# Weights turned by f32 transpositions, the first head's weights and tiles first, the experts' weights turned and folded in the first six periods

## The reference

```python
xn = _layernorm(x, axis=-1)                       # x: 8 x 1024 x 128
Q = einsum('bnd,hdk->bhnk', xn, proj_q)           # 8 heads
K = einsum('bmd,dk->bmk', xn, proj_k)
V = einsum('bmd,dv->bmv', xn, proj_v)
weights = softmax(einsum('bhnk,bmk->bhnm', Q, K), axis=-1)
Y = einsum('bhnv,hdv->bnd', einsum('bhnm,bmv->bhnv', weights, V), proj_o)
ffn = einsum('aemn,enh->amh', einsum('amh,ehn->aemn', xn, w1), w2)   # w1: 8 x 128 x 512
out = x + Y + ffn
```

## Time and profile before

| | |
|---|---|
| median of 3 runs | 1669.72 us |
| profiled execution | 1669.67 us, span 1667.9 us |
| ScalarE busy | 1304.2 us (78%) |
| VectorE busy | 1239.3 us (74%) |
| GpSimd busy | 1379.9 us (83%) |
| first matmul | 5.77 us into the span |
| first `high_pass` | 24.92 us |
| DMA | near full for some 30 us, then about 1% |

### The profile page before, as it was taken

The page is one execution under the profiler, slowest core; times in us unless marked ns, Lnnn a source line. Parts: engine busy times, 40 slices in busy tenths (PEclk is TensorE's granted clock), DMA queues, the critical chain, the costliest instruction groups (busy, mean ns, idle before and its releaser), DMA issues.

```text
span 1667.9 us, 46510 instructions
## 1 busy us (share of the span) xinstructions
PE 1634.7 (98%) x18820; PEld 1214.1 (73%) x18820; DVE 1239.3 (74%) x2655; ACT 1304.2 (78%) x1350; POOL 1379.9 (83%) x1008
## 2 busy tenths in 40 slices
PE   7999999999999999999999999999999999999998
PEld 6777777777777777777777777777777777777775
DVE  5777777777777777777777777777777777777775
ACT  4777877787787788778778777877878787787785
POOL 2788888888888888888888888888888888878876
PEclk9999999999999999999999999999999999999999
DMA  8000000000000000000000000000000000000000
GB/s 230 2 2 2 1 2 14 2 2 2 2 15 2 2 2 3 13 2 2 2 8 8 2 2 1 8 8 2 2 2 8 8 2 2 2 14 2 2 1 14
DMA packets 16769, 16.73 MB, mean 10 GB/s; under 512 B 432, under 2 KB 12976, under 8 KB 16560
## 3 DMA queue, kind: packets, MB, share of 16 engines
q1 hardware_dynamic: 15520, 13.24, 2.7%
q10 hardware_dynamic: 1040, 0.52, 0.1%
HBM read 9.57 MB, written 4.19 MB: 8 GB/s over the span
## 4 chain that ended last, share of the span: by engine, by line
POOL 56%; issue 24%; PE 18%; ACT 1%; DVE 0%; POOLq 0%; DMA 0%; SPq 0%; DVEq 0%; ACTq 0%
POOL pr_lo L306 40%; POOL xacc L318 9%; POOL xn L300 3%; PE s_ps L548 2%; PE s_ps L550 2%; PE s_ps L535 2%; PE t_ps L586 2%; PE t_ps L589 2%; PE t_ps L588 2%; POOL rstd L345 2%; POOL xacc L324 1%; POOL xn_lo L290 1%; PE s_ps L432 1%; PE s_ps L434 1%; PE s_ps L433 1%
## 5 line engine op out<-in xcount | busy, mean ns | idle before, releaser
L306 POOL TENSOR_TENSOR pr_lo<-pr,pr_hi 128x1024 f16<-128x1024 f32 x511 | 1086.4, 2134 | 264.3 <-ACT pr_hi L396 264.3
L389 ACT ACTIVATE pr<-s_ps,boost,scale 128x1024 f32<-128x1024 f32 x512 | 616.8, 1205 | 211.1 <-PE s_ps L550 210.3
L778 DVE TENSOR_REDUCE key_max<-s_ps 128x128 f16<-128x1024 f32 x512 | 624.0, 1219 | 0.0
L396 ACT ACTIVATE pr_hi<-pr 128x1024 f16<-128x1024 f32 x512 | 525.4, 1051 | 8.1
L548 PE MATMUL s_ps<-g_lo,xT 128*128 128x128 f16 x4096 | 512.4, 219 | 1.1 <-DVE g_lo L791 1.1
L550 PE MATMUL s_ps<-g_hi,xT 128*128 128x128 f16 x4096 | 512.3, 219 | 0.0
L548 PEld LDWEIGHTS s_ps<-g_lo,xT 128*128 128x128 f16 x4096 | 400.7, 98 | 31.6 <-DVE g_lo L791 1.6
L550 PEld LDWEIGHTS s_ps<-g_hi,xT 128*128 128x128 f16 x4096 | 400.8, 98 | 29.7
L586 PE MATMUL t_ps<-pr_hi,xn_hi 128*128 128x512 f16 x1024 | 388.7, 380 | 16.3 <-POOL pr_lo L306 14.4
L588 PE MATMUL t_ps<-pr_lo,xn_hi 128*128 128x512 f16 x1024 | 388.1, 379 | 0.0
L589 PE MATMUL t_ps<-pr_hi,xn_lo 128*128 128x512 f16 x1024 | 388.1, 379 | 0.0
(11 more groups left out here) (123 smaller groups left out, 1602.7 us busy)
## 6 DMA issues: line engine op xcount, KB each, us to landing
out_dram<-xacc SPq DMA_DIRECT2D x16, 256.0 KB, 2.3
w_sb<-in_L_ffn_w_dram SPq DMA_DIRECT2D x1, 2048.0 KB, 10.2
pr<-in_L_attn_proj_q_dram ACTq DMA_DIRECT2D x1, 512.0 KB, 4.7
xacc<-in_L_attn_x_dram SPq DMA_DIRECT2D x2, 256.0 KB, 5.1
pr<-in_L_attn_proj_o_dram SPq DMA_DIRECT2D x1, 512.0 KB, 6.5
xacc<-in_L_attn_x_dram SPq DMA_DIRECT2D x1, 384.0 KB, 11.0
xacc<-in_L_attn_x_dram SPq DMA_DIRECT2D x1, 128.0 KB, 6.3
wkv<-in_L_attn_proj_k_dram SPq DMA_DIRECT2D x1, 64.0 KB, 2.9
```

The costliest lines, as they stand in the source:

```text
L306: pool.tensor_tensor(pr_lo[:, u % RING, :], pr32[:, u % PR, :], pr_hi[:, u % RING, :], ALU.subtract)\
L389: act.activation(pr32[:, u % PR, :], both_banks(u), ACT.Exp, bias=boost[:, 0:1], scale=scale[:, 0:1])\
L396: act.activation(pr_hi[:, u % RING, :], pr32[:, u % PR, :], ACT.Copy).then_inc(p_hi_ready, 1)
L778: dve.tensor_reduce(key_max[:, u % 2, :], both_banks(u).rearrange("p (t q) -> p q t", q=P), AX_X, ALU.max).then_inc(keys_max, 1)
```

## The change

- Query, output and w1 weights are turned by `pe.transpose` with the f32 identity instead of f32 matmuls. The centring is then done elsewhere: for the query weights on VectorE, which copies the turned first columns of the heads (`wq_first`) and subtracts them while emptying PSUM (ScalarE's copy L368 goes); for the experts once, by one f32 matmul of F with `centre` in period 7, with a second copy of F.
- TensorE's prologue: the output weights are turned behind fold A; fold C is split in two halves, one ahead of `project(0)`, one in period 0; tiles 0 to 3 are turned ahead of `row_of_amax`; tiles 4 to 7 behind `project(0)`; no expert is turned in the prologue.
- ScalarE splits one head of A high first, the other seven behind the first `g_high`; C is copied in two halves. GpSimd makes the low half of tiles 0 to 3 as well. VectorE's order is changed to suit.
- All 8 experts are turned in periods 0 to 3, two in each, through one PSUM bank; all 8 are folded in periods 4 and 5, four in each, in the other bank. F's largest is found in period 8.

```diff
-        def w1_turn(e):
-            return s_ps[:, (2 + e % 2) * BANK:(3 + e % 2) * BANK] if e < 3 else sum_bank(-2)
+        def c_ps(half):
+            return s_ps[:, (2 + half) * BANK:(3 + half) * BANK]
+        W1_BANK, FOLD_BANK = 0, 1
+        FOLDS = {4: 0, 5: 1}
@@ GpSimd
+            first_rstd(0)
+            first_rstd(1)
+            xn_low(0, 0, HT)
             xn_low(HT, HT, HT)
+            first_rstd(2)
@@ ScalarE
-            act.wait_ge(transposed, 2)
-            act.activation(wqT, s_ps[:, 0:N].rearrange("p (h k) -> p h k", h=H), ACT.Copy).then_inc(evacuated, 1)
-            split_high(0, 0, HT)
             act.wait_ge(transposed, 3)
             act.activation(woT, s_ps[:, N:2 * N], ACT.Copy).then_inc(evacuated, 1)
+            split_high(0, 0, HT)
             split_high(HT, HT, HT)
-            act.wait_ge(folded, 2)
-            act.activation(c32[:, :], s_ps[:, N:2 * N], ACT.Copy).then_inc(c_copied, 1)
             act.wait_ge(scales, 1)
-            act.activation(a_hi[:, :, :], a_ps.rearrange("p (h k) -> p h k", h=H), ACT.Copy,
-                           scale=inv_scale[:, 0:1]).then_inc(hi_ready, 1)
-            for e in range(3):
-                empty_w1(e)
+            high_of_a(0, 1)
+            empty_c(0)
             g_high(0)
+            high_of_a(1, H - 1)
+            empty_c(1)
             for n in range(PERIODS):
-                if n < 3:
-                    empty_w1(2 * n + 3)
+                if n < 4:
+                    empty_w1(2 * n)
...
                     exponentials(n - 1)
-                if n < 2:
-                    empty_w1(2 * n + 4)
+                if n < 4:
+                    empty_w1(2 * n + 1)
@@ TensorE
             for h in range(H):
-                last = pe.matmul(s_ps[:, h * P:(h + 1) * P], wq_sb[:, h, :], centre[:, :], start=True, stop=True)
-            last.then_inc(transposed, 1)
-            pe.wait_ge(o_in, 16)
-            for h in range(H):
-                last = pe.matmul(s_ps[:, N + h * P:N + (h + 1) * P], wo_sb[:, h, :], ident[:, :], start=True, stop=True)
+                last = pe.transpose(s_ps[:, h * P:(h + 1) * P], wq_sb[:, h, :], ident[:, :])
             last.then_inc(transposed, 1)
...
             last.then_inc(folded, 1)
+            pe.wait_ge(o_in, 16)
+            for h in range(H):
+                last = pe.transpose(s_ps[:, N + h * P:N + (h + 1) * P], wo_sb[:, h, :], ident[:, :])
+            last.then_inc(transposed, 1)
@@ turn_w1(e)
                 for c in range(MC):
-                    last = pe.matmul(w1_turn(e)[:, c * P:(c + 1) * P], w1_sb[:, e, c * P:(c + 1) * P], centre[:, :],
-                                     start=True, stop=True)
+                    last = pe.transpose(sum_bank(W1_BANK)[:, c * P:(c + 1) * P], w1_sb[:, e, c * P:(c + 1) * P], ident[:, :])
@@ max_to_row(u)
+                if u == 3:
+                    pe.wait_ge(w1_evacuated, E)
@@ chunk(n, place)
+                if n < 4 and rest:
+                    turn_w1(2 * n + place)
+                if n in FOLDS and rest:
+                    for e in range(2):
+                        fold_ffn(4 * FOLDS[n] + 2 * place + e)
@@ small_products(n)
+                if n == F_CENTRED:
+                    pe.wait_ge(f_copied, 1)
+                    pe.matmul(ffn_part(n), centre[:, :], f32w[:, :], start=True, stop=True).then_inc(f_ps, 1)
@@ TensorE's order
-            row_of_amax(0, None)
             turn_tiles(0)
+            row_of_amax(0, None)
             spread_amax(0, None)
-            turn_w1(0)
-            turn_tiles(HT)
-            turn_w1(1)
+            fold_c(0)
             pe.wait_ge(weights_ready, 1)
             project(0)
-            turn_w1(2)
+            turn_tiles(HT)
             for n in range(PERIODS):
...
+                if n == 0:
+                    fold_c(1)
                 chunk(n, 0)
@@ VectorE
             tile_stats(0)
+            wq_turned = s_ps[:, 0:N].rearrange("p (h d) -> p h d", h=H)
+            dve.wait_ge(transposed, 2)
+            dve.tensor_copy(wq_first[:, :], wq_turned[:, :, 0]).then_inc(wq_first_ready, 1)
+            dve.wait_ge(wq_first_ready, 1)
+            dve.tensor_tensor(wqT, wq_turned, wq_first[:, :].unsqueeze(2).to_broadcast([P, H, P]), ALU.subtract)\
+               .then_inc(evacuated, 1)
+            tile_means(0)
             tile_stats(1)
+            tile_means(1)
             normalise_first(0)
...
             dve.wait_ge(folded, 1)
             find_amax(0, a_ps)
+            normalise_first(1, 0, 2)
             reduce_amax(0, None)
+            normalise_first(1, 2, 4)
             power_of_two(0, None)
+            copy_first(0)
             low_of_a(0, 1)
+            tile_stats(2)
+            tile_means(2)
+            copy_first(HT)
```

More of the change, by code:

```diff
@@ L169, in attention_ffn, with first_turned @@
         a_ps = s_ps[:, 4 * BANK:6 * BANK]
-        def w1_turn(e):
-            return s_ps[:, (2 + e % 2) * BANK:(3 + e % 2) * BANK] if e < 3 else sum_bank(-2)
+        def c_ps(half):
+            return s_ps[:, (2 + half) * BANK:(3 + half) * BANK]
+        def first_turned(first):
+            return (t_ps[:, BANK:2 * BANK] if first == 0 else s_ps[:, 3 * BANK:4 * BANK]).bitcast(F16)
         def summing(n):
@@ L239, in ffn_part @@
             return bank(n + 1, 0)[:, 0:D]
+        F_CENTRED = 7
         def turned_part(n):
@@ L279, in _, with first_rstd @@
             pool.memset(centre[0:1, 0:1], 0.0).then_inc(consts, 1)
-            for g, (first, count) in enumerate(FIRST_TILES):
+            def first_rstd(g):
+                first, count = FIRST_TILES[g]
                 pool.wait_ge(ln_var, g + 1)
@@ L364, in empty_w1, with high_of_a, empty_c @@
                 act.wait_ge(w1_turned, e + 1)
-                act.activation(w1T[:, e, :], w1_turn(e), ACT.Copy).then_inc(w1_evacuated, 1)
-            act.wait_ge(transposed, 2)
-            act.activation(wqT, s_ps[:, 0:N].rearrange("p (h k) -> p h k", h=H), ACT.Copy).then_inc(evacuated, 1)
-            split_high(0, 0, HT)
+                act.activation(w1T[:, e, :], sum_bank(W1_BANK), ACT.Copy).then_inc(w1_evacuated, 1)
+            def high_of_a(first, count):
+                heads = a_ps.rearrange("p (h k) -> p h k", h=H)[:, first:first + count, :]
+                act.activation(a_hi[:, first:first + count, :], heads, ACT.Copy, scale=inv_scale[:, 0:1])\
+                   .then_inc(hi_ready, 1)
+            def empty_c(half):
+                act.wait_ge(folded, half + 2)
+                act.activation(c32[:, half * BANK:(half + 1) * BANK], c_ps(half), ACT.Copy).then_inc(c_copied, 1)
             act.wait_ge(transposed, 3)
             act.activation(woT, s_ps[:, N:2 * N], ACT.Copy).then_inc(evacuated, 1)
+            split_high(0, 0, HT)
             split_high(HT, HT, HT)
-            act.wait_ge(folded, 2)
-            act.activation(c32[:, :], s_ps[:, N:2 * N], ACT.Copy).then_inc(c_copied, 1)
             act.wait_ge(scales, 1)
-            act.activation(a_hi[:, :, :], a_ps.rearrange("p (h k) -> p h k", h=H), ACT.Copy,
-                           scale=inv_scale[:, 0:1]).then_inc(hi_ready, 1)
-            for e in range(3):
-                empty_w1(e)
+            high_of_a(0, 1)
+            empty_c(0)
             def g_high(k):
@@ L453, in _, with fold_c @@
             last.then_inc(folded, 1)
[L454 to L458, removed]
+            pe.wait_ge(o_in, 16)
+            for h in range(H):
+                last = pe.transpose(s_ps[:, N + h * P:N + (h + 1) * P], wo_sb[:, h, :], ident[:, :])
+            last.then_inc(transposed, 1)
+            def fold_c(half):
+                pe.wait_ge(evacuated, 2)
+                if half == 1:
+                    pe.wait_ge(xT_ready, NT)
+                pe.matmul(c_ps(half), wkvT[:, P:2 * P], woT[:, half * BANK:(half + 1) * BANK], start=True, stop=True)\
+                  .then_inc(folded, 1)
             def turn_tiles(first):
@@ L515, in high_pass @@
                     if u == 1:
-                        pe.wait_ge(w1_evacuated, 3)
+                        pe.wait_ge(c_copied, 1)
+                    if u == F_CENTRED + 1:
+                        pe.wait_ge(f_copied, 2)
                     if u - 1 in SPREAD:
@@ L596, in fold_ffn @@
                     pe.wait_ge(w1_evacuated, E)
+                    pe.wait_ge(max_found, 4)
+                    pe.wait_ge(bias_ready, 3)
                 for c in range(MC):
-                    last = pe.matmul(sum_bank(-1)[:, 0:D], w1T[:, e, c * P:(c + 1) * P], w2_sb[:, e, c, :],
+                    last = pe.matmul(sum_bank(FOLD_BANK)[:, 0:D], w1T[:, e, c * P:(c + 1) * P], w2_sb[:, e, c, :],
                                      start=e == 0 and c == 0, stop=e == E - 1 and c == MC - 1)
@@ L727, in low_of_a @@
                 heads = a_ps.rearrange("p (h k) -> p h k", h=H)[:, first:first + count, :]
-                dve.wait_ge(hi_ready, 1)
+                dve.wait_ge(hi_ready, 1 if first == 0 else 2)
```

(19 more changed lines are left out.)

49 lines of the change are left out of this document (25 added, 24 removed).

## The result

The changed kernel takes 1672.95 us in the median of 16 runs (1671.16 to 1674.76), the kernel before 1669.18 us (16 runs, 1668.60 to 1670.30). The ratio is 1.0021, 95% interval 1.0014 to 1.0029. The forecast was 1671.3, range 1667.8 to 1674.6. The profiled execution took 1673.30 us, span 1671.5.

What follows compares the result with a forecast made beforehand. TensorE was taken to bound the kernel, with everything decided in the first 50 us. The prologue's -1.2 us and the periods' +2.85 us summed to +1.65 us, giving 1671.3 us, range 1667.8 to 1674.6.

Steps and rivals of the forecast that it cites:

- K: Start of the first reduction over keys, 25.58 us in the kernel before; forecast at 24.4, 1.2 us earlier.
- E(5): Start of unit 5's exponential; its shift is the end's shift. Prediction wrong if it comes before 48 or after 54.
- What bounds, and where the time is decided: Whole kernel: TensorE busy 98% of the span; the steady stretch from 60 us keeps its length, the first 50 us decide.
- Price of an f32 transposition: TensorE's turns of 128 x 128 weights: 0.112 us taken each, between bounds 0.056 and 0.224.
- lower-price rival: Weight turns on TensorE: 0.056 us a transposition, -1.8 us, time 1669.5, with a full clock 1667.7; chance 0.20.
- rival of 0.224 us: Weight turns on TensorE: f32 transposition costs what the f32 product costs, +3.8 us, time 1675.1; chance 0.10.
- Periods 0 to 3 and 4 to 6: After the prologue: first fold at K + 15.3, then TensorE alone for 12.85 us; bunching the folds loses 2.85 us.
- E(0): Start of unit 0's exponential, forecast at K + 5.7; the numbers 1 and 2 mean units 1 and 2, K + 8.95 and 13.25.
- gapless rival: Early periods lose nothing: TensorE's 22.6 us from K to E(5) run without gaps, time 1664; chance 0.06.
- Prologue: Chain of weight work ahead of K: K 3.0 us earlier at 22.6, less 1.8 us for one clock fall.
- Fold A: 1.79, 10.3 to 12.1: Prologue step on TensorE: fold A takes 1.79 us, from 10.3 to 12.1, 1.1 us earlier than before.
- The clock stays low longer: Prologue: fold A at half clock, 1.1 us more, time 1672.4; with a second fall in periods 0 to 3, 1674.1; chance 0.17.

Runs made afterwards that it cites:

- w1_matmul: Changed kernel with w1 turned by f32 matmuls with the identity instead of transpositions; median 1674.92 us, ratio 1.0034 to the kernel before.
- bunched: Kernel before with only the folds' places changed: four in each of periods 4 and 5, none in 2, 3 and 6; median 1670.53 us, ratio 1.0008.
- dve_copies: Changed kernel with the w1 copies of experts 5 and 7 (periods 2 and 3) on VectorE instead of ScalarE; median 1671.81 us, ratio 1.0015.
- fill_start: Changed kernel with only 30 filler matmuls ahead of the key weights' arrival; median 1671.10 us, ratio 1.0009 to the kernel before.
- fill_pause: Changed kernel with only 14 filler matmuls in TensorE's pause between turned query weights and fold A; median 1671.96 us, ratio 1.0015 to the kernel before.
- q_matmul: Changed kernel with the query weights turned by f32 matmuls with the identity, first columns still subtracted on VectorE; median 1672.49 us, ratio 1.0017 to the kernel before.
- before_fill: Kernel before plus filler f16 matmuls: 30 ahead of the key weights, 24 before tiles 4 to 7 are turned; median 1667.65 us, ratio 0.9992.
- fill_matmul: Changed kernel plus 70 f16 filler matmuls: 30 ahead of the key weights, 14 ahead of fold A, 26 ahead of the first tiles' turn; median 1669.03 us.
- w1_only: Kernel before with w1 turned by f32 transpositions in the old places and F centred by one f32 matmul in period 7; median 1668.12 us, ratio 0.9994.

## Why the prediction was right, and where it was off

The time fell inside the stated range, on the forecast side of the kernel before, and periods 0 to 6 went as forecast. The prologue did not: K was to come 1.2 us earlier and came 0.63 later. The range held because its upper part allowed for a longer low clock. The prediction's own sign of being wrong, E(5) after 54, came true by a little (54.30). And 3.8 us is more than the 3.3 that it took as distinguishable, an outcome (slower) to which it gave 0.16.

**What bounds, and where the time is decided: right.** The steady stretch is unchanged, and time less E(5) is constant within 0.5 us over fourteen kernels.

**Price of an f32 transposition: right.** 0.112 taken, 0.111 measured. The Trainium skill (TensorE: Matmul & The Clock Gate, Terms) has the transposition mode four times faster for f32; here it is twice as fast as the f32 matmul (0.224 us), so the lower-price rival is out. So is the rival of 0.224 us: w1_matmul shows what the w1 turns alone would have cost. (By its own terms that rival would pass +3.3 from 0.16 a transposition, not 0.17.)

**Periods 0 to 3 and 4 to 6: right.** K + 5.7, 8.95, 13.25, first fold 15.3, E(5) 28.15 were forecast; 5.63, 9.07, 13.02, 15.14 and 28.09 came. Two errors cancel in part, which is luck: E(0) to E(1) took 3.44 (3.25 forecast), E(1) to E(2) 3.95 (4.3). The loss from K to E(5) is 2.78 us (2.85 forecast). bunched shows 1.25 of it as the folds' place alone. dve_copies gives back 0.63 for two of ScalarE's copies. If the two add up, which was not tried, about 0.9 is left; it would lie in the other turns and copies that the periods took over from the prologue, and was not taken apart further. The gapless rival is out.

**Prologue: mis-sized, by the clock.** The forecast had K at 24.4, 1.2 us ahead of before; it was 26.21, 0.63 behind. The step "Fold A: 1.79, 10.3 to 12.1" is where it went: 10.08 to 13.83. The step took for granted that the clock rises by 8.75 as before; it rose at about 14.4 in the profiled execution. Of the 1.96 us too much, 1.73 is the clock (3.75 against 2.02 at the full clock), and 0.23 is that fold A behind a pause takes 2.02, not 1.79, even then. With the output weights' turn (1.25 against 0.9) TensorE is 2.1 late at 15.08 against the forecast's 13.0, and 1.8 of it is carried on to K. That is the rival "The clock stays low longer", priced there at 1.1 us. The low clock later in the prologue was in the forecast with 1.8 us, for a fall at 15.6, which came at about 17.8. Filling the pauses gives 3.9 us of medians, so about half of what the low clock cost was foreseen.

**The mechanism behind that rival: not as named.** It leaned on transpositions not holding the clock. The Trainium skill (TensorE: Matmul & The Clock Gate, Part 4) says so; for f16 transpositions the runs disagree (1669.13 with them, 1669.03 with matmuls, and fold A at full speed behind 30 of them). What the runs show is that more work of TensorE ahead of fold A has the clock up for it: 30 fillers at the start (fill_start), 14 in the pause (fill_pause), or the longer query turn of q_matmul with no filler and the pause left open, fold A 2.02 in each. So the pause alone is not what kept the clock low; it was the pause together with how little ran ahead of it. Whether an f32 transposition counts less than an f32 matmul of the same length was not tried by itself, and stays open.

**The sum.** +1.65 was forecast, +3.6 to +3.8 measured: 0.6 from the prologue, 2.8 from the periods, and 0.2 in the profiled executions that no part here accounts for (twelve other kernels do not show it).

## What to carry to other kernels

A kernel that TensorE bounds is shortened by taking work off TensorE only where nothing else sets the pace. Work moved from a prologue into periods must meet idle time of the same engine there, and heavy pieces were better spread than bunched here (1.25 us). In a prologue of short dependent steps, price each TensorE step at both clock levels, and ask of each pause that an edit opens whether the clock outlasts it; a few useless matmuls in the pauses are a cheap test, and here a gain.

## What was not expected of the hardware

- Useless work pays: 70 filler operations of 128 columns took 3.9 us off the changed kernel, 54 of them 1.65 off the kernel before (before_fill).
- The scatter goes with the low clock, as far as seen. The 16 runs of the changed kernel lie 3.6 us apart, the 16 of the kernel before 1.7, the 11 of before_fill, whose profiled execution has 1.00 in every stretch, 0.5 (1667.53 to 1668.06). Fillers do not always bring that: the 11 runs of fill_matmul lie 2.0 apart.
- A faster TensorE step may bring the clock down later: in its profiled execution w1_only fell again in its first period, behind a stretch with 1.91 of 3.4 us busy, where the kernel before stayed at 1.00 with 2.12. That the shorter turns were the reason is argued from these two executions, not shown.
